# Attention over a context: half of the value tiles as three reduced-precision products, two context buffers, and one row queue

## What is computed

```python
x = x + tanh(g_xattn) * softmax(layernorm(x) @ ctx.T) @ ctx       # per batch: 100 x 722 scores
x = x + tanh(g_ffn) * (layernorm(x) @ dequantize(qweight).T + bias)   # all 800 rows, 2048 x 2048
```

## Time and profile before

| | us |
|---|---|
| median of 3 runs | 633.53 |
| profiled execution | 630.83 |
| its span | 628.3 |
| PE busy | 598.9 (95%) |
| DVE busy | 393.0 (63%) |
| ACT busy | 195.9 (31%) |
| POOL busy | 58.3 (9%) |

### The profile page before, as it was taken

How to read it: one execution, slowest core, us unless ns; L and a number is a source line. 1 busy time by engine, 2 the same in 40 slices (tenths; PEclk the granted TensorE clock), 3 DMA queues, 4 the chain that set the end, 5 groups by cost and what they waited for, 6 DMA issues and landing times.

```text
span 628.3 us, 8137 instructions
## 1 busy us (share of the span) xinstructions
PE 598.9 (95%) x3240; PEld 385.9 (61%) x3240; DVE 393.0 (63%) x687; ACT 195.9 (31%) x391; POOL 58.3 (9%) x149
## 2 busy tenths in 40 slices
PE   0988999999999999999999999999999999999997
PEld 0877965964884894794695696454555444444442
DVE  2675654673666767667667567778686663773533
ACT  1544522531450451451351353233232130220000
POOL 3010010013004004004002102020100000000000
PEclk9997999999899999999999999999999999999999
DMA  8999828318907926935940582978661797593311
GB/s 253 278 310 263 232 90 289 112 54 293 207 35 230 247 110 206 268 114 166 280 141 1 149 344 79 260 276 180 203 212 48 207 278 180 133 222 90 104 55 38
DMA packets 39618, 113.64 MB, mean 181 GB/s; under 512 B 20974, under 2 KB 20974, under 8 KB 29422
## 3 DMA queue, kind: packets, MB, share of 16 engines
q1 hardware_dynamic: 18718, 83.54, 44.0%
q0 software_dynamic: 4224, 25.40, 13.6%
q10 hardware_dynamic: 16640, 4.20, 4.4%
HBM read 89.26 MB, written 19.66 MB: 173 GB/s over the span
## 4 chain that ended last, share of the span: by engine, by line
PE 87%; DMA 6%; DVE 3%; ACT 1%; SPq 1%; issue 0%; POOL 0%; DVEq 0%; POOLq 0%
PE pv L820 23%; PE pv L871 18%; PE S L801 13%; PE T L762 10%; PE S L871 9%; PE S L803 7%; PE pv L762 6%; DMA raw<-in_ctx 5%; DMA xres<-in_x 2%; DVE stats L532 1%; PE T L844 1%; PE S L884 1%; PE pv L884 1%; SPq L234 1%; DVE xres L566 0%
## 5 line engine op out<-in xcount | busy, mean ns | idle before, releaser
L820 PE MATMUL pv<-raw,pT 128*100 128x512 f32 (+1 forms) x384 | 170.5, 594 | 2.5 <-ACT pT L444 2.5
L801 PE MATMUL S<-khi,qT 128*100 128x362 f32 x512 | 143.2, 361 | 0.0
L820 PEld LDWEIGHTS pv<-raw,pT 128*100 128x100 f32 (+1 forms) x384 | 61.8, 167 | 88.9 <-issue 85.1
L871 PE MATMUL pv<-raw 128*128 128x512 f16 x448 | 98.5, 379 | 0.0
L674 DVE TENSOR_TENSOR klo<-T,khi 128x361 fp32r<-128x361 f32 x128 | 67.7, 533 | 36.0 <-ACT khi L429 35.3
L803 PE MATMUL S<-klo,qT 128*100 128x362 f32 x256 | 85.9, 335 | 1.5 <-DVE klo L674 1.5
L674 DVE TENSOR_TENSOR klo<-pv,khi 128x361 fp32r<-128x361 f32 x128 | 67.6, 533 | 30.6 <-ACT khi L429 30.3
L429 ACT ACTIVATE khi<-T 128x361 fp32r<-128x361 f32 x128 | 59.9, 473 | 66.7 <-PE T L762 66.6
L871 PEld LDWEIGHTS pv<-raw 128*128 128x128 f16 x448 | 43.5, 98 | 52.5 <-issue 1.7
L429 ACT ACTIVATE khi<-pv 128x361 fp32r<-128x361 f32 x128 | 60.1, 475 | 39.3 <-PE pv L762 38.8
L762 PE MATMUL T<-ident,raw 128*128 128x128 f32 (+1 forms) x432 | 69.0, 277 | 3.5 <-DMA raw<-in_ctx 2.3
(11 more groups left out here) (80 smaller groups left out, 461.0 us busy)
## 6 DMA issues: line engine op xcount, KB each, us to landing
raw<-in_ctx SPq DMA_DIRECT2D x32, 1024.0 KB, 15.5
raw<-in_ctx SPq DMA_DIRECT2D x16, 840.0 KB, 16.5
raw<-in_L_ffn_qweight SPq DMA_DIRECT2D x16, 768.0 KB, 7.2
xres<-in_x POOLq DMA_DIRECT2D x8, 800.0 KB, 8.1
x_scratch<-xres POOLq DMA_DIRECT2D x8, 800.0 KB, 13.5
rows_scratch<-rows POOLq DMA_DIRECT2D x8, 800.0 KB, 12.6
raw<-x_scratch SPq DMA_DIRECT2D x24, 256.0 KB, 4.1
out_y<-raw SPq DMA_DIRECT2D x24, 256.0 KB, 2.5
```

The costliest lines, as they stand in the source:

```text
L801: pe.matmul(S[0:R, g, 0:MW], qT[:, h, c, :], khi[:, slot, :], start=(c == 0 and h == 0), stop=False)
L820: last = pe.matmul(pv[n][0:R, :], pT[0:ROWS[t], t, :], raw[0:ROWS[t], b % 3, t, n * 512:(n + 1) * 512], start=(t == 0), stop=(t == NT - 1))
L871: last = pe.matmul(ACC[j % NA][0:r, :], xT[m][:, h, c, :], WT[nb % 2][:, c, :], start=(c == 0 and h == 0), stop=(c == CH - 1 and h == 1))
```

## The change

1. **Products in halves.** `HALVED = 3`: the first three tiles of each batch are split into `vhi` (ACT, `context_hi`) and `vlo` (POOL, `context_lo`), the transposed exponentials into `ph[:, 0]` (ACT) and `ph[:, 1]` (DVE, `probs_lo`). PE makes three float32r products in place of the float32 one. `vhi` and `vlo` hold three tiles: tile t of batch b+1 is written when PE has used tile t of batch b.
2. **Order.** `probs(i)` moves from behind `scores(i+1)` into its middle (before chunk 16); `probs(7)` into `attend(6)`.
3. **Two context buffers** in place of three (`raw[:, b % 2]`). A tile of batch b+2 is loaded once `vlo` of batch b is made (tiles 0 to 2) or PE has used it (tiles 3 to 5).
4. **Normalizations on ACT**: `ln1_norm` and `ln2_norm` are one scaled and shifted copy each; POOL gets two more one-column operations per `rstd`; the buffer `rows` goes, and there are two `xres`.
5. **One queue**: all row transfers but `rs_out` move from POOL's queue to SP's, between the context loads.
6. **The start of the second layer is reordered**, and the loads of `scB`, `cB`, `bB` (1 MB each) now wait until tile 2 of `attend(7)` is done, since their place was a context buffer and is now that of `vhi` and `vlo`; `load_w(4)` stands behind them.

```diff
+                if t < HALVED:
+                    sp.wait_ge(s_vlo, b * HALVED + t + 1)
...
+            for b in range(2, B):
+                next_x(b)
+                if b >= 3:
+                    x1_out(b - 3)
+                for t in range(HALVED):
+                    used(b - 2, t)
+                    load_ctx(b, t)
+                if b >= 4:
+                    next_xres(b - 2)
+                for t in range(HALVED, NT):
+                    used(b - 2, t)
+                    load_ctx(b, t)
+                    if t == HALVED and b >= 3:
+                        rows_out(b - 3)
...
+            load_w(3)
+            sp.wait_ge(s_pvt, LAST * (NT - 1) + HALVED)
+            sp.dma_start(scB, ...)
+            sp.dma_start(cB, ...)
+            sp.dma_start(bB, ...)
+            load_w(RT)
...
+            def context_lo(b, t):
+                r = ROWS[t]
+                pool.wait_ge(s_vhi, b * HALVED + t + 1)
+                pool.tensor_tensor(vlo[0:r, t, :], raw[0:r, b % 2, t, :], vhi[0:r, t, :].bitcast(F32),
+                                   ALU.subtract).then_inc(s_vlo, 1)
...
+            def context_hi(b, t):
+                if b >= 1:
+                    act.wait_ge(s_pvt, (b - 1) * (NT - 1) + t + 1)
+                act.activation(vhi[0:ROWS[t], t, :], raw[0:ROWS[t], b % 2, t, :], ACT.Copy).then_inc(s_vhi, 1)
...
-                if i < LAST:
-                    context(i + 1)
-                    probs(i)
-                    exps(i + 1)
+            for i in range(LAST):
+                keys_hi(i + 1, {CH: lambda: probs(i)})
+                exps(i + 1)
+                context_hi(i + 1, 0)
+                if i + 2 < B:
+                    ln1_norm(i + 2)
+                context_hi(i + 1, 1)
+                context_hi(i + 1, 2)
+                if i + 2 < B:
+                    queries(i + 2, (0, 1))
+                if i >= 1:
+                    ln2_norm(i - 1)
+                if i + 2 < B:
+                    queries(i + 2, (2, 3))
...
-                        last = pe.matmul(pv[n][0:R, :], pT[0:ROWS[t], t, :], raw[0:ROWS[t], b % 3, t, n * 512:(n + 1) * 512],
-                                         start=(t == 0), stop=(t == NT - 1))
...
+                        for a, (p, v) in enumerate(((0, vhi), (0, vlo), (1, vhi))):
+                            if t == 0 and p == 1:
+                                written("P", b, 0)
+                            for n in range(NCH):
+                                if t == 0 and a == 0 and b >= 1:
+                                    pe.wait_ge(s_x1, (b - 1) * NCH + n + 1)
+                                last = pe.matmul(pv[n][0:R, :], ph[0:r, p, t, :], v[0:r, t, n * 512:(n + 1) * 512],
+                                                 start=(t == 0 and a == 0), stop=False)
...
-                scores(i + 1)
-                probs(i)
+                scores(i + 1, {CH: lambda: probs(i)})
...
+                    attend(i, {3: lambda: normed(0, (0, 1)), 4: lambda: normed(0, (2, 3)), 5: lambda: probs(LAST)})
+            attend(LAST, {1: lambda: weights(0), 2: lambda: weights(1), 3: lambda: normed(1, (0, 1)),
+                          4: lambda: normed(1, (2, 3)), 5: lambda: weights(2)})
+            weights(3)
+            multiply(0, 0, {5: lambda: normed(2, (0, 1)), 11: lambda: normed(2, (2, 3))})
```

More of the change, by code:

```diff
@@ L76, in flamingo_block @@
         xa = sb("xa", [P, D])
-        xres = sb("xres", [P, D])
-        rows = sb("rows", [P, D])
+        xres = [sb(f"xres{k}", [P, D]) for k in range(2)]
         E = sb("E", [P, 2, GW])
-        pT = sb("pT", [P, NT, R])
+        ph = sb("ph", [P, 2, HALVED, R], F32R)
+        pT = sb("pT", [P, NT - HALVED, R])
         ident = sb("ident", [P, P])
@@ L286, in _ @@
             load_rows(0)
+            x1_out(LAST - 2)
+            used(LAST - 1, 0)
+            load_w(0)
+            next_xres(LAST - 1)
+            used(LAST - 1, 1)
+            used(LAST - 1, 3)
+            load_w(1)
+            rows_out(LAST - 2)
+            load_w(2)
             load_rows(1)
-            for n in range(2):
-                sp.wait_ge(s_pvt, (LAST - 1) * (NT - 1) + n + 1)
-                load_w(n)
+            used(LAST, 2)
             load_rows(2)
-            load_w(2)
+            next_xres(LAST)
+            x1_out(LAST - 1)
             load_w(3)
+            sp.wait_ge(s_pvt, LAST * (NT - 1) + HALVED)
+            sp.dma_start(scB, wscale.rearrange("n o -> (n o)").partition_broadcast(P)).then_inc(s_scB, 16)
+            sp.dma_start(cB, wzero.rearrange("n o -> (n o)").partition_broadcast(P)).then_inc(s_cB, 16)
+            sp.dma_start(bB, wbias.partition_broadcast(P)).then_inc(s_bB, 16)
+            load_w(RT)
             load_rows(3)
-            load_w(RT)
+            rows_out(LAST - 1)
             load_w(RT + 1)
-            load_rows(4)
-            load_w(RT + 2)
             sp.wait_ge(s_rsout, 16 * LAST)
@@ L305, in _ @@
                 load_x1(j)
+            x1_out(LAST)
+            load_w(RT + 2)
+            load_rows(4)
+            rows_out(LAST)
             load_w(RT + 3)
@@ L401, in _ @@
                 if i >= 1:
-                    next_xres(i)
-                    rows_out(i - 1)
                     rs_out(i - 1)
-            x1_out(LAST)
             rstd(1, LAST)
-            rows_out(LAST)
             rs_out(LAST)
@@ L487, in _ @@
             queries(0)
-            context(0)
+            keys_hi(0, {20: lambda: context_hi(0, 0), 24: lambda: context_hi(0, 1), 28: lambda: context_hi(0, 2)})
             act.wait_ge(s_gate, 32)
@@ L722, in _ @@
             ln2_stats(LAST)
-            ln2_center(LAST)
-            ln2_scale(LAST)
+            rows_lo(2, 0)
+            scale_and_bias()
+            rows_lo(2, 1)
+            shares()
             rows_lo(3, 0)
+            before(0)
             rows_lo(3, 1)
             unpack(RT + 1)
-            before(0)
+            after(0)
             rows_lo(4, 0)
             before(1)
-            after(0)
+            after(1)
             rows_lo(4, 1)
@@ L734, in _ @@
             before(2)
-            after(1)
-            before(3)
             after(2)
             unpack(RT + 3)
+            before(3)
             rows_lo(5, 0)
```

343 lines of the change are left out of this document (185 added, 158 removed).

## The result

| | before | after |
|---|---|---|
| median, us (lowest to highest, 4 runs each) | 632.09 (629.45 to 635.8) | 660.98 (651.23 to 672.93) |
| profiled execution, us | 630.83 | 660.9 |
| its span, us | 628.3 | 659.1 |
| mean granted TensorE clock | 0.991 | 0.961 |
| PE busy, us | 598.9 | 593.0 |

The changed kernel is slower: the ratio is 1.039 (95% interval 1.027 to 1.052), where the forecast was a gain of 2%.

What follows compares the result with a forecast made beforehand. PE's own list was taken to bound the kernel (87% of the chain). The terms -19.1 + 6.2 - 1.3 - 3.5 + 8 = -9.7 us, against the profiled 630.8, gave 621 us, range 608 to 640.

Steps and rivals of the forecast that it cites:

- Parts 3 to 5: Start and transfers: -1.3 us in `scores(0)`, -3.5 us from two `xres`, later context tiles in time.
- the tile is wanted at S+35: in time, with 4 us left: Context tiles at chunk 16, S being the start of `attend(i)`: tiles and write take 12 to 14 us from S+17.
- the one queue late: Write ahead of tile 5 on SP's queue makes it 4 us late in five batches: +28 us, 649; chance 12%.
- The start: In `scores(0)`: a 2.33 us tile wait goes, three ACT copies add 1.0: -1.3 us (-2.3 to +2).
- POOL's pass: POOL's subtraction of 2048 columns in `attend(i)`: at 4 us hidden, no cost; PE waits above about 7 us.
- the rival of a pass over 7 us: POOL's subtraction at 10 us makes PE wait 3 us in each of 6 batches: 649 us; chance 6%.
- Part 6: Start of the second layer, E being the start of `attend(7)`: waits and lower clock cost +8 us (+1 to +15).
- The wait for T0: In `multiply(0, 0)`: PE waits 4.5 us (1.5 to 10) for bank T0, behind the late load of `w4`.
- Part 1: 96 float32 matmuls become 288 float32r ones of 0.225 us each: 19.1 us less (16.8 to 21.7).
- Part 2: `probs` inside the scores: 1.25 us of waiting 7 times, less 2.5 us saved: net +6.2 us (+4 to +9).
- The clock rival: Each `probs` wait is followed by 3 us at 1.2 GHz, 1.5 us lost, 7 times: 632 us; chance 12%.
- The wait for `xres`: The residual's 2.35 us wait behind `next_xres(1)`, and the low clock after it, go with two `xres`: -3.5 us.

Runs made afterwards that it cites:

- C4: C3 with `rows_out` ahead of tile 4 again: 641.6 us (10 runs), ratio 1.011.
- C3: C1 with `probs` back behind the scores: 617.9 us (4 runs), ratio 0.980.
- E3: Changed kernel with `rows_out` behind tile 5 instead of ahead of tile 4: 638.2 us, ratio 1.0105.
- E5: Changed kernel with `rows_out` of batches 0 to 4 started from ACT's queue, at the same moment: 636.6 us, ratio 1.009.
- E1: Changed kernel with POOL's three subtractions of batch 0 waiting until DVE has done `ln1_norm(1)`: 657.7 us median of 4, no ratio.
- F1: E3 and E1 together: 625.4 us, ratio 0.992.
- E6: Changed kernel with POOL's subtractions cut from 2048 columns to 16, the rest of `vlo` zero: 643.6 us, ratio 1.019.
- E2: Changed kernel with SP's wait for `rs_out` and load of `rs_all` moved behind `load_rows(4)`: 655.9 us median of 4, no ratio.
- E4: Changed kernel with `ln2_norm(5)` on ACT moved between the halves of `rows_hi(0)`: 658.1 us, ratio 1.031.
- C2: C1 with one plain float32 product of the upper halves in place of three float32r ones: 636.8 us (7 runs), ratio 1.011.
- C1: F1 with E4's order, `ln2_norm(6)` ahead of `weights(2)`, `load_w(4)` ahead of the 1 MB loads, `x1_out(LAST)` and `load_rows(4)` ahead of the `rs_out` wait: 620.7 us, ratio 0.988.
- C5: C3 with `before(0)` on DVE behind `rows_lo(3, 1)` and `unpack(5)`: 615.6 us (6 runs), ratio 0.974.

## Why the prediction was wrong

**Parts 3 to 5, "the tile is wanted at S+35: in time, with 4 us left": the step that failed.** In the changed kernel S is 142.25, and `attend` ended at S+19.9, as forecast (timeline of PE, the first block of `scores(3)`):

```profile
162.17 0.79 PE L846 MATMUL T<-ident,raw 128*128 128x128 f32 x6
```

Tile 5 was issued at S+20.1, since PE has used it only at the end of `attend`; I had let all of the traffic start at S+17. It landed 16.35 us later, at S+36.5, where I had 29 to 31. And PE wanted it at 174.41, S+32.2, not 35: from the end of `attend` to chunk 16 it takes 12.2 us, where I had put about 15. Three errors in one direction, 3 us in the issue, over 2 in the landing and 3 in the moment it is wanted, ate the margin of 4 us and 4 more. The rival for this, the one queue late, was priced at 28 us; C4 against C3 measures 20, and E3 and E5 against the changed kernel 18 and 19 with a shorter wait for the rows in them. Its chance of 12% was too small: the margin of 4 us was hardly larger than the spread of the landing time (13.06 to 16.83 us in the five batches).

**The start, -1.3 forecast, +9.7 measured.** The forecast costed POOL's pass by the gaps it may leave on POOL and ACT, and asked only in `attend` what stands near it. In `scores(0)` it runs beside DVE's `ln1_norm(1)`, which goes from 1.34 to 9.68 us; PE waits 7.74 and loses some 3 more to the clock. No step and no rival named this. E1, F1 and E6 show by order and by length that POOL's pass is the cause; how it keeps DVE out no run shows. The Trainium skill has the rule in "SBUF — State Buffer", section "SBUF: two separate sides": DVE and GpSimd share a pair of ports under an exclusive lock held for a whole instruction; the two rows of E1 agree, and the row of E3 shows that DVE may be kept out through three instructions of POOL in succession.

**POOL's pass.** Taken at 4 us, waiting from 7 on; it is 4.68 on average (5.49 for the first one of `attend(6)`). In the batches it is hidden, as forecast, and the rival of a pass over 7 us did not hold. What was missed is `attend(6)`, where `rows_hi(0)` stands behind `ln2_norm(5)` on ACT: 3.79 us and the clock. The term that I had worked out from `attend(i)` was not looked at again in the one `attend` with another list behind it.

**Part 6, +8 forecast.** The wait for T0 (4.5 us, 1.5 to 10) did not show in the profile of the changed kernel, only because PE was held up before. It is there in others: 2.27 in E2, 7.36 in E4, 10.45 in E6. E3 has 0.35, F1 1.44 and E5 2.74. So the mechanism was right, and the wait goes a little beyond both bounds. The lower one had an error in it: 3.9 MB at 421 GB/s from E+9.9 on are there at E+19.2 and not at 22.5, and by the same list PE would not wait at all. What took its place was the queue's next item, `load_rows(4)`, priced at 1.5 us and measured at 12.37. I had counted the bytes ahead of it on SP's queue and not the wait ahead of it on SP: a transfer of 0.4 KB from POOL's queue that takes 12.2 us to land, and right behind it the landing of `rows_out(6)`. What the first costs by itself is not measured: without it the load is issued 3.5 us earlier (E2), and the wait came out at 3.69 and 2.67 us in E3 and E5 with the order as it was.

**Part 1, the products.** Right in mechanism; the size was 0.2295 each in place of 0.225, 17.8 us for 19.1. C2 confirms it in the time, with 16.2 us.

**Part 2, `probs`.** 0.97 us a batch in place of 1.25, near my lower bound of 0.9; net 7 x 0.97 - 2.5 = +4.3 for +6.2, and C3 measures 4.2 in the periods. The clock rival did not hold: in C1, with seven such waits, the mean clock is 0.990.

**The wait for `xres`** The earlier trace rows is gone, as forecast.

**The terms that failed all lay on one side.** The edits are cheap or good; what they did to the order on SP's queue and in ACT's list, and to DVE beside POOL's pass, was not. With these mended the same edits are 1.2% faster than before (C1), without the move of `probs` 2.0% (C3), and with `before(0)` later 2.6% (C5).

## What to carry to other kernels

When buffers become fewer or queues are joined, work out for each load when its place becomes free, when it is wanted and what is ahead of it in its queue; if the margin is not clearly larger than the spread of its landing time, put writes behind it (E3) or on another queue (E5). Ask of every operation given to POOL which DVE operation runs at the same moment in each stage, the first one too, and of every wait on a queue's engine what loads stand behind it. A mended wait brings PE earlier to the next load, as in E4 and E6, so take the moments at which loads are wanted from the new schedule.

## What the runs showed of the hardware

- DVE's `tensor_scalar` on 100 x 2048 float32 took 1.34 us alone and 9.68 and 14.19 us when begun 0.5 us behind the first of three subtractions on POOL. DVE's `klo` operations, which read PSUM and SBUF, kept their 533 ns beside the same subtractions.
- A write of 0.8 MB ahead of two loads in one queue made tiles late that were on time with the write behind them (ratio 1.011 for 0.980, C4 and C3) or at the same moment in a second hardware queue (1.039 for 1.009, changed kernel and E5).
- A transfer of 0.4 KB on POOL's queue took 12.3 us to land (median of 8) beside a busy hardware queue.
- float32r products of 512 columns: 0.2295 us each; the plain float32 ones 0.874, and 0.858 in C2.
- The granted clock fell at gaps of 2.27 us and more in the changed kernel and not after 1.39, 1.22 and 0.97. That is no fixed bound: before, it stayed at 1.00 after one of 2.33 and fell after 0.38 and 0.90 within 2.5 us, and in E6 it was 1.00 after 2.24 and 1.96 and 0.68 after 2.02.
